# Cross-attention with float32r split products: the order of the SBUF allocations, matmul weights first and streamed operands 64 bytes (modulo 128) off them

## The reference

```python
Q = (img_embed @ Wq).reshape(B, -1, H, D).transpose(0, 2, 1, 3)
K = (sent_embed @ Wk) ...   # the same shape
V = (sent_embed @ Wv) ...
score = jnp.einsum('bhqd,bhkd->bhqk', Q, K) / math.sqrt(D)
attn = jax.nn.softmax(where(mask, score, -inf), axis=-1)
ctx = jnp.einsum('bhqk,bhkd->bqhd', attn, V).reshape(B, -1, H * D)
out = ctx @ Wo + img_embed
return (out - mu) * jax.lax.rsqrt(var + EPS) * gamma + beta    # over the last axis
```

## Time and profile before

| | us |
|---|---|
| median of 3 runs (327.90 to 328.21) | 327.98 |
| the profiled execution | 327.89 |
| its span, first to last instruction | 326.1 |
| PE busy in it | 316.7 (97%) |
| PE weight loads busy | 294.7 (90%) |
| DVE busy | 253.4 (78%) |
| ACT busy | 222.0 (68%) |
| POOL busy | 180.7 (55%) |
| granted TensorE clock, mean | 0.998 |

### The profile page before, as it was taken

The page is one execution under the profiler, slowest core; times in us unless marked ns, Lnnn a source line. Parts: engine busy times, 40 slices in busy tenths (PEclk is TensorE's granted clock), DMA queues, the critical chain, the costliest instruction groups (busy, mean ns, idle before and its releaser), DMA issues.

```text
span 326.1 us, 7399 instructions
## 1 busy us (share of the span) xinstructions
PE 316.7 (97%) x2264; PEld 294.7 (90%) x2264; DVE 253.4 (78%) x721; ACT 222.0 (68%) x601; POOL 180.7 (55%) x183
## 2 busy tenths in 40 slices
PE   8999998999999999999999999999999999998992
PEld 7998887999999999999999999999999999997792
DVE  0557868777998879977997789977997799765685
ACT  2456668678866887668767787778766877666450
POOL 1123358457864486458755686448754785546201
PEclk9999999999999999999999999999999999999999
DMA  7995433464345634364356425455347334530000
GB/s 258 362 409 188 146 114 131 153 208 133 127 128 178 190 130 139 138 213 145 113 185 209 150 83 177 157 169 165 118 143 235 132 129 140 170 104 10 24 32 32
DMA packets 46910, 50.26 MB, mean 154 GB/s; under 512 B 3504, under 2 KB 37040, under 8 KB 46896
## 3 DMA queue, kind: packets, MB, share of 16 engines
q1 hardware_dynamic: 46608, 49.56, 45.7%
q10 hardware_dynamic: 288, 0.52, 0.6%
HBM read 32.24 MB, written 17.83 MB: 154 GB/s over the span
## 4 chain that ended last, share of the span: by engine, by line
PE 87%; DVE 4%; ACT 3%; POOL 2%; DMA 2%; issue 1%; SPq 1%; POOLq 0%; DVEq 0%
PE score_bank L312 22%; PE out_bank L312 19%; PE gL_bank L312 13%; PE tL_bank L312 12%; PE tU_bank L312 8%; PE gU_bank L312 6%; DMA wq_raw<-in_wqT 2%; PE tL_bank L346 1%; PE spare_bank L346 1%; DVE tU L785 1%; PE tL_bank L328 1%; PE tU_bank L328 1%; POOL pT_lo L983 1%; ACT tL_hi L528 1%; PE tU_bank L352 1%
## 5 line engine op out<-in xcount | busy, mean ns | idle before, releaser
L960 POOL TENSOR_TENSOR probs<-probs,inv_sum 128x512 f32<-128x512 f32 x64 | 66.6, 1042 | 88.9 <-DVE inv_sum L748 88.2
L571 ACT ACTIVATE probs<-neg_scores,neg_max 128x256 f32<-128x256 f32 x128 | 64.3, 504 | 32.3 <-DVE neg_max L737 32.2
L983 POOL TENSOR_TENSOR pT_lo<-pT_raw,pT_hi 128x512 fp32r<-128x512 f32 x60 | 76.3, 1292 | 11.6 <-ACT pT_hi L528 11.6
L737 DVE CUSTOM_DVE_ANT_0 neg_scores<-score_bank,mask_bias 128x256 f32<-128x256 f32 x128 | 49.2, 421 | 7.4 <-PE score_bank L312 4.5
L528 ACT ACTIVATE tL_hi<-tL_bank 128x512 fp32r<-128x512 f32 x31 | 18.5, 597 | 40.2 <-PE tL_bank L312 40.2
L758 DVE STREAM_TRANSPOSE squares<-probs 128x512 f32<-128x512 f32 x60 | 42.3, 706 | 0.3
L685 DVE TENSOR_TENSOR tL_lo<-tL_bank,tL_hi 128x512 fp32r<-128x512 f32 x31 | 21.3, 688 | 24.7 <-ACT tL_hi L528 24.6
L312 PE MATMUL score_bank<-ctxT_hi,gU 128*128 128x256 f32 x128 | 36.5, 285 | 0.7 <-POOL ctxT_lo L972 0.7
L312 PE MATMUL score_bank<-ctxT_hi,gL_lo 128*128 128x256 f32 x128 | 36.3, 283 | 0.0
L312 PE MATMUL score_bank<-ctxT_hi,gL_hi 128*128 128x256 f32 x128 | 36.2, 283 | 0.0
L312 PE MATMUL score_bank<-ctxT_lo,gL_hi 128*128 128x256 f32 x128 | 36.2, 283 | 0.0
(11 more groups left out here) (166 smaller groups left out, 951.5 us busy)
## 6 DMA issues: line engine op xcount, KB each, us to landing
scratch<-squares SPq DMA_DIRECT2D x30, 512.0 KB, 2.8
pT_raw<-scratch SPq DMA_DIRECT2D x120, 128.0 KB, 3.1
xT_raw<-in_xT SPq DMA_DIRECT2D x8, 256.0 KB, 4.5
ctxT_raw<-in_ctxT SPq DMA_DIRECT2D x8, 256.0 KB, 4.7
wo_raw<-in_wo SPq DMA_DIRECT2D x4, 512.0 KB, 14.1
x_res<-in_x SPq DMA_DIRECT2D x8, 256.0 KB, 2.9
out<-y_out SPq DMA_DIRECT2D x7, 256.0 KB, 2.8
wq_raw<-in_wqT SPq DMA_DIRECT2D x3, 512.0 KB, 7.5
```

The costliest lines, as they stand in the source:

```text
L571: nc.scalar.activation(probs[j % 2][:, n, :], neg_scores[:, n, :], ACT.Exp, bias=neg_max[:, n:n + 1], scale=-1.0, accum_out=row_sum[:, n:n ...
L737: nc.vector.tensor_tensor_reduce(out=neg_scores[:, n, :], in0=score_bank[hh][:, q, :], in1=mask_bias[:], scale=-SCALE, scalar=3.0e38, op0= ...
L960: nc.gpsimd.tensor_tensor(probs[j % 2][:, rows, :], probs[j % 2][:, rows, :], inv, ALU.mult) \
L983: nc.gpsimd.tensor_tensor(pT_lo[j % 2][:, k].rearrange("p hh (q i r) -> p (hh q) i r", q=QT, i=ROWS), pT_raw[j % 2][:, k].rearrange("p i n ...
```

## The change

The `sb(...)` calls are put in another order; no shape, instruction, wait or loop is changed. Behind A_lo now come all tiles that are weights of L312 (ctxL_hi, ctxL_lo, ctxU, gL_hi, gL_lo, gU, tL_hi, tL_lo, tU_hi, tU_lo), then eps_col and power_col, which move the start by 64 bytes, then all streamed tiles, then the rest.

```diff
         A_hi = sb("A_hi", [P, IT, PAIRS * PW], F32R)
         A_lo = sb("A_lo", [P, IT, PAIRS * PW], F32R)
+        ctxL_hi = sb("ctxL_hi", [P, KT, P], F32R)
+        ctxL_lo = sb("ctxL_lo", [P, KT, P], F32R)
+        ctxU = sb("ctxU", [P, KT, 2 * UP], F32R)
+        gL_hi = sb("gL_hi", [P, 2, S], F32R)
+        gL_lo = sb("gL_lo", [P, 2, S], F32R)
+        gU = sb("gU", [P, 2, S], F32R)
+        tL_hi = sb("tL_hi", [P, 2, S], F32R)
+        tL_lo = sb("tL_lo", [P, 2, S], F32R)
+        tU_hi = sb("tU_hi", [P, S], F32R)
+        tU_lo = sb("tU_lo", [P, S], F32R)
+
+        eps_col = sb("eps_col", [P, QT])
+        power_col = sb("power_col", [P, QT])
+
+        xT_hi = sb("xT_hi", [P, IT, S], F32R)
+        xT_lo = sb("xT_lo", [P, IT, S], F32R)
+        ctxT_hi = sb("ctxT_hi", [P, 2, KV], F32R)
+        ctxT_lo = sb("ctxT_lo", [P, 2, KV], F32R)
         CL_hi = sb("CL_hi", [P, H, DI], F32R)
         CL_lo = sb("CL_lo", [P, H, DI], F32R)
         CU_hi = sb("CU_hi", [P, PAIRS, DI], F32R)
         CU_lo = sb("CU_lo", [P, PAIRS, DI], F32R)
+        pT_hi = [sb(f"pT_hi{n}", [P, KT, 2, S], F32R) for n in range(2)]
+        pT_lo = [sb(f"pT_lo{n}", [P, KT, 2, S], F32R) for n in range(2)]
...
-        neg_max = sb("neg_max", [P, 2 * QT])
...
-        row_sum = sb("row_sum", [P, 2 * QT])
-        inv_sum = sb("inv_sum", [P, 2 * QT])
...
         mean_var = sb("mean_var", [P, QT, 2])
+        neg_max = sb("neg_max", [P, 2 * QT])
+        row_sum = sb("row_sum", [P, 2 * QT])
+        inv_sum = sb("inv_sum", [P, 2 * QT])
```

More of the change, by code:

```diff
@@ L67, in attention_kernel @@
         zeros = sb("zeros", [P, DI])
-        eps_col = sb("eps_col", [P, QT])
-        power_col = sb("power_col", [P, QT])
         xT_raw = sb("xT_raw", [P, IT, S])
-        xT_hi = sb("xT_hi", [P, IT, S], F32R)
-        xT_lo = sb("xT_lo", [P, IT, S], F32R)
         ctxT_raw = sb("ctxT_raw", [P, 2, KV])
-        ctxT_hi = sb("ctxT_hi", [P, 2, KV], F32R)
-        ctxT_lo = sb("ctxT_lo", [P, 2, KV], F32R)
         ctx_raw = sb("ctx_raw", [P, KT, DL])
-        ctxL_hi = sb("ctxL_hi", [P, KT, P], F32R)
-        ctxL_lo = sb("ctxL_lo", [P, KT, P], F32R)
-        ctxU = sb("ctxU", [P, KT, 2 * UP], F32R)
         mask_raw = sb("mask_raw", [P, KV], I32)
@@ L84, in attention_kernel @@
         x_res = sb("x_res", [P, QT, DI])
-        gL_hi = sb("gL_hi", [P, 2, S], F32R)
-        gL_lo = sb("gL_lo", [P, 2, S], F32R)
-        gU = sb("gU", [P, 2, S], F32R)
         neg_scores = sb("neg_scores", [P, 2 * QT, KV])
-        neg_max = sb("neg_max", [P, 2 * QT])
         probs = [sb(f"probs{n}", [P, 2 * QT, KV]) for n in range(2)]
-        row_sum = sb("row_sum", [P, 2 * QT])
-        inv_sum = sb("inv_sum", [P, 2 * QT])
         squares = sb("squares", [P, SQUARES, 2 * QT, SQ])
         pT_raw = [sb(f"pT_raw{n}", [P, KT, ROWS, 2 * QT, SQ]) for n in range(2)]
[L96 to L99, removed]
         tU_moved = sb("tU_moved", [P, S])
         tU = sb("tU", [P, S])
-        tU_hi = sb("tU_hi", [P, S], F32R)
-        tU_lo = sb("tU_lo", [P, S], F32R)
         y = sb("y", [P, QT, DI])
```

## The result

The changed kernel takes 326.99 us (median of 6 runs, 326.66 to 327.17) against 328.03: ratio 0.9965, interval 0.9955 to 0.9976. That is 1.0 us faster where 8.7 were forecast. All ratios in this document are to the kernel before, run beside the kernel in question.

What follows compares the result with a forecast made beforehand. The prediction took PE to bound the loop, as matmuls times the distance between starts. Gains of 8.2 (loop), 0.25 (start) and 0.23 us (tail) sum to 8.7, from 327.89 to 319.2 us; range 316.8 to 322.0.

Steps and rivals of the forecast that it cites:

- Bound by PE, the time is the number of matmuls times their distance: In the loop, 27 steps, 241 of 326 us: only the distance between matmul starts can be changed by tile places.
- Query products: In each loop step: tiles 64 against 0 before and after, so 113.3 ns each and no change.
- Scores and output products: In each loop step: 20 scores and 18 output products drop to 113.3 ns, 0.12 us less for each kind.
- step 30: In the tail: output products from xT slow to some 119.5 ns, hidden by a DVE wait, 0.07 us at most; gU stays fast.
- Context products: In each loop step: ten 512-column products lose 6.5 ns each, to 226.5 ns, 0.065 us less a step.
- the upper bound: For the ten 512-column products: each loses 2 x 6.5 = 13 ns, 0.13 us a step; as a rival, 317.5 us, chance 0.14.
- Start: Before the loop: three earlier score pieces on the chain gain between 0 and 0.36 us, taken as 0.25.
- slack of 0.80 us in the layer-norm steps: DVE's margin before PE needs gL_lo: the change uses 0.57 us, so no stall and 0.23 left.
- the sum of addresses that counts is longer than 7 bits: Rival for the loop: new places are among the bad ones, 0.18 us more a step, 332.8 us; chance 0.02.
- An unchanged 328.0, because the places are of no account: Rival for the whole kernel: tile places do not matter and the time stays at 328.0 us; chance 0.03.
- The forecast of a step, 8.62: Length in us of one loop step after the change, 0.305 less than before.

Runs made afterwards that it cites:

- apart192: Changed kernel with a pad of 128 bytes more between weights and streamed tiles, so 192 apart modulo 256 instead of 64: 321.24 us, ratio 0.9793.
- all_apart0: Changed kernel with eps_col and power_col moved behind stats, so weights and streamed tiles all start at 0 modulo 128: 330.32 us, ratio 1.0072.
- fourth_in_halves: Changed kernel with the fourth context product made as two of 256 columns instead of one of 512, same work and addresses: 320.55 us, ratio 0.9769.
- products_more: Matmuls only, attention left out: stretches each begun behind a restart, with various distances and numbers of 512-column products; executed once, 243.2 us.
- context11: Changed kernel with one extra 512-column product, 64 apart, behind the ten context products of each step from 4 on: 330.01 us, ratio 1.0062.
- context12: Changed kernel with two extra 512-column products, 64 apart, behind the ten context products of each step from 4 on: 333.08 us, ratio 1.0155.
- g_at64: Changed kernel with gL_hi, gL_lo and gU allocated at 64 again, so the scores are 0 apart as in the kernel before: 323.61 us, ratio 0.9864.
- products: Matmuls only, attention left out: stretches at various distances and widths, each distance followed by products 64 apart; executed once, 128.67 us.

## Why the prediction was wrong

- *Bound by PE, the time is the number of matmuls times their distance*: right. PE is busy 97% of the span before and after, at a granted clock of 0.998 and 0.995, the chain is PE from step to step, and 27 times the change of a step (0.035) gives 0.95 us. The two profiled spans differ by 0.7 (326.1 and 325.4): the loop begins 0.29 us later, at 52.67 instead of 52.38.
- *Query products: "64 against 0 before and after, no change"*: this step failed. They went from 113.3 to 117.7 with no operand at another distance, 18 x 4.4 ns = 0.08 us a step lost, 2.1 us in all.
- *Scores and output products: 20 x 113.3 and 18 x 113.3*: the same error. They came to 117.7, 0.035 and 0.04 less a step and not 0.12 each. The evidence compared xT and gU at 64 with tL at 32 correctly, but both the query products and step 30 were seen in one state only, behind scores 0 apart or in the fast phase of the tail. Step 30 was no test of the new places either: CL at 0 behind weights at 64 is 192 apart modulo 256, the distance of apart192, not the 64 of the changed kernel. The state was hidden in the kernel before: each 64-apart stretch of its loop was entered from scores 0 apart. One stretch was not, the first query products, which stand behind folds. In the chain of the kernel before their twelve of gL_bank took 1.41 and not 1.36, 117.5 ns each, and I did not use that row:

```profile
15.19 1.41 PE gL_bank L312 x12
```

- *Context products: one drop of 6.5 ns to 226.5*: 2.30 for the ten in the changed kernel, 230 each, so 0.03 to 0.04 a step against 0.065. They gained more than nothing and less than the 0.13 of the upper bound. What a 512-column stream takes without the loads of weights beside it, no run shows.
- *Start, 0.25 gained*: failed with the query products. From the landing of the first weights to the score piece of step 4 there are 43.36 us before (9.02 to 52.38) and 43.48 after (9.19 to 52.67), 0.12 more; scores and query products of steps 0 to 2 stood at 117.7. The other 0.17 of the later start is the transfer of wq_raw, 6.48 against 6.30.
- *Step 30 at 119.5 from xT, gU fast, no stall of DVE, other engines unchanged*: the step 30 pair came out (120 and 114), no wait is new, the large DVE and POOL groups are within 1%. The slack of 0.80 us in the layer-norm steps held 0.75 in the changed kernel, and it would have had to give more in apart192, where 0.35 is left.
- *Rivals*: "the sum of addresses that counts is longer than 7 bits" was right as a fact (0 and 128, 112 and 240 with matmuls alone) and wrong as a price. None of them was what happened, a second state of the same pair of addresses. An unchanged 328.0, because the places are of no account (chance 0.03), was not it either: in all_apart0 the 64 bytes less cost 3.3 us.
- The forecast of a step, 8.62, is what fourth_in_halves runs at (8.63). That the distance of the tiles counts was right (all_apart0), and the mechanism priced the stream at 113.3; what was missing was what decides between 113.3 and 117.7.

The place of the two tiles counts with matmuls alone as well: behind the same kind of restart, 256-column products settled at 120 ns with the tiles 0 apart and at 113.3 with them 112 apart (products_more). That the read of the moving tile and the load of the next weights get into each other's way was my reading of the earlier trace rows; no run shows that the time is lost in reading SBUF.

Shown: the two states, that they need no other engine, and that with all pairs 64 apart the state follows the end of the 512-column cycle, in matmuls alone and in the kernel; edits that changed this end (context11, context12, fourth_in_halves) changed the state with it. Not shown: what the phase physically is (the traces give starts of matmuls, not of the reads of SBUF); what sets the entry of the 512-column products behind a slow stream; why products 0 apart leave the stream fast in the attention kernel (the kernel before, g_at64) and slow in matmuls alone; and why 112 apart is fast from a restart. That distance was not tried in the kernel.

## What to carry to other kernels

When every float32r product has its own weight load and TensorE is the bound, look at the distance between starts (113.3 to 120 ns here), not at busy times (276 to 286), and try weights and streamed tiles 64 bytes apart modulo 128, which was worth 3.3 us of 330 here. Then check the trace for the slower of the two distances: a product at 117.7 whose twin elsewhere runs at 113.3. If it is there, change what stands before the stretch (one 512-column product in two halves, or tiles 192 bytes apart in place of 64), look again, and don't take one stretch's distance as the price of a pair of addresses until it has been seen behind several neighbours.

## What the runs showed of the hardware

- Each matmul has a weight load of its own: the pages of before and after count 2264 MATMUL and 2264 LDWEIGHTS. In the groups of before, by form, `LDWEIGHTS score_bank<-ctxT_hi,gU 128*128 128x128` (busy 190 ns, 128 columns of the stationary tile gU) stands beside the MATMUL of the same name with a moving tile of 128x256, and the context products have one of 128x512. In the loop of before (52.38 to 293.60) PE is busy all of the 241.22 us and the loads 228.85 of them, so they run beside the matmuls.
- A float32r product with its own load of 128 weight columns never cost under 111 ns on average: 111.6 for 128 columns, 111.6 for 192, 113.3 to 120 for settled stretches of 256. In products the means then grow: 146.7 for 320 columns, 173.3 for 384 (26.6 ns for 64 columns more) and 229.0 for 512 (55.7 for 128 more).
- Products at fixed addresses can have two stable speeds, 4% apart (113.3 and 117.7), each of them held through a loop of 230 us (fourth_in_halves and the changed kernel); the times of each kernel's runs agree within 0.9 us. An added 512-column product made a kernel slower by less than its own cost (context11 330.0: one more in each step, 3.0 us over the changed kernel where 27 x 0.23 = 6.2 went in).
- Restarts behind a wait mostly began slow, at 117.7, for products 64 apart (all six in the first kernel of products); in the changed kernel one of the first five score stretches, at 44.55, began fast, at 113.2.
